# Routed experts of a two-layer model: second products two steps behind, the next expert's tokens turned inside the current expert

## The reference, cut to what matters

```python
xt = x.reshape(n, h)                       # n = 4096, h = 256
S = jax.nn.sigmoid(xt @ Wg).T              # 8 experts
G, I = jax.lax.top_k(S, k)                 # k = 1024 tokens for each expert
ex = xt[I]
hid = jax.nn.gelu(jnp.einsum('ekh,ehf->ekf', ex, W1) + b1[:, None, :], approximate=False)   # f = 1024
out = (jnp.einsum('ekf,efh->ekh', hid, W2) + b2[:, None, :]) * G[..., None]
new_x = jnp.zeros_like(xt).at[I.reshape(-1)].add(out.reshape(-1, h))
```

## Time and profile before

| | us |
|---|---|
| median of 3 runs | 4653.36 |
| lowest, highest | 4644.17, 4657.75 |
| profiled execution: its time | 4639.34 |
| profiled execution: span from first to last instruction | 4637.6 |
| stage `ae`, first `up` to last `down` | 416.79 |
| stage `ce`, the same | 420.58 |

### The profile page before, as it was taken

One profiled execution on the slowest core, in us unless ns is written; L12 is line 12 of the kernel. 1 busy time (PEld: TensorE's weight loads), 2 busy tenths in 40 slices (PEclk: granted clock), 3 DMA queues, 4 the chain that ended last, 5 costly groups with the idle time before them and its releaser, 6 DMA issues. The chain is left out here.

```text
span 4637.6 us, 74096 instructions
## 1 busy us (share of the span) xinstructions
PE 4047.9 (87%) x26222; PEld 3129.6 (67%) x26222; DVE 2729.8 (59%) x5268; ACT 1988.4 (43%) x3960; POOL 566.3 (12%) x428
## 2 busy tenths in 40 slices
PE   4599949989974599968999969999999997799999
PEld 3488835555544588857888856666566664788888
DVE  4544446665645544437777756655666555577777
ACT  1555524544440555512333336555655554133332
POOL 0144321211200144210000000000000000000000
PEclk6699968999995799969999979999999999699999
DMA  3243220000003343220000020000000001000001
GB/s 113 89 93 82 30 57 6 24 20 16 24 25 100 100 85 80 29 56 11 14 10 11 6 77 6 10 11 11 1 10 10 11 6 38 18 11 14 10 14 36
DMA packets 144876, 159.23 MB, mean 34 GB/s; under 512 B 20320, under 2 KB 132704, under 8 KB 144352
## 3 DMA queue, kind: packets, MB, share of 16 engines
q1 hardware_dynamic: 117728, 113.15, 7.5%
q0 software_dynamic: 26880, 42.48, 5.0%
HBM read 105.01 MB, written 50.59 MB: 34 GB/s over the span
## 5 line engine op out<-in xcount | busy, mean ns | idle before, releaser
L1895 ACT ACTIVATE e_prob<-e_s_ps,e_small 128x512 f32<-128x512 f32 x512 | 346.7, 685 | 173.2 <-PE e_t_ps L1785 88.2
L2006 DVE TENSOR_REDUCE e_small<-e_s_ps 128x2 f32<-128x1024 f32 x256 | 313.3, 1224 | 170.8 <-PE e_s_ps L1772 166.6
L1312 ACT ACTIVATE b_pt<-b_t_ps 128x1024 f32<-128x1024 f32 (+3 forms) x256 | 180.9, 706 | 305.0 <-PE b_t_ps L1244 304.0
L1785 PE MATMUL e_t_ps<-const,e_prob 128*128 128x128 f32 x2048 | 267.9, 274 | 9.5 <-ACT e_pt L1884 5.3
L1806 PE MATMUL e_z_ps<-e_pt,e_v 128*64 128x512 f32 x1024 | 275.5, 617 | 0.4 <-DVE e_zf L2086 0.4
L1984 POOL TENSOR_TENSOR e_wide<-e_small,const 128x512 f32<-128x512 f32 x64 | 66.5, 1039 | 1708.4 <-DVE e_small L2079 1708.4
L1785 PEld LDWEIGHTS e_t_ps<-const,e_prob 128*128 128x128 f32 x2048 | 234.1, 141 | 55.8 <-issue 22.5
L1495 DVE TENSOR_REDUCE b_small<-b_s_ps 128x2 f32<-128x1024 f32 (+3 forms) x256 | 209.8, 820 | 85.1 <-PE b_s_ps L1223 81.1
L942 DVE SCALAR_TENSOR_TENSOR d_xs<-d_o_ps,d_coef,d_xs 128x256 f32<-128x256 f32 x576 | 238.1, 476 | 1.3 <-PE d_o_ps L62 1.3
L942 DVE SCALAR_TENSOR_TENSOR f_xs<-f_o_ps,f_coef,f_xs 128x256 f32<-128x256 f32 x576 | 238.1, 476 | 1.3 <-PE f_o_ps L62 1.3
L60 PE MATMUL f_h_ps<-f_x_hi,f_w_hi 128*128 128x512 f32 x576 | 227.5, 395 | 0.0
(11 more groups left out here) (540 smaller groups left out, 11757.0 us busy)
## 6 DMA issues: line engine op xcount, KB each, us to landing
ae_raw<-w_dram SPq DMA_DIRECT2D x16, 1024.0 KB
ce_raw<-w_dram SPq DMA_DIRECT2D x16, 1024.0 KB
d_raw<-m_dram SPq DMA_DIRECT2D x54, 128.0 KB, 2.2
f_raw<-m_dram SPq DMA_DIRECT2D x54, 128.0 KB, 2.2
b_xs<-x_dram SPq DMA_DIRECT2D x9, 512.0 KB, 3.8
ar_xs<-x_dram SPq DMA_DIRECT2D x8, 512.0 KB, 9.3
x_dram<-ar_xs SPq DMA_DIRECT2D x8, 512.0 KB, 7.6
rows_dram<-ar_xn POOLq DMA_DIRECT2D x8, 512.0 KB, 4.7
```

What stands on the lines that cost most here:

```text
L1312: act.activation(pt[:, kt % 2, a, :, 0:width], t_ps[:, :, 0:width], ACT.Exp).then_inc(p_ready, 1)
L1785: last = pe.transpose(t_ps[:, h, kt * P:(kt + 1) * P], prob[:, bank_of(s) + h, kt * P:(kt + 1) * P], ident)
L1895: act.activation(prob[:, at], s_ps[:, at], ACT.Exp, bias=nmx[:, at:at + 1], accum_out=sums[:, buf, h * QT + s:h * QT + s + 1]).then_inc(p_ ...
L2006: dve.tensor_reduce(nmx[:, at:at + 2], s_ps[:, at:at + 2], AX.X, ALU.max, negate=True).then_inc(mx_ready, 1)
```

## The change

PE does `down(n-2)` after `up(n)`; the last two `down` of an expert stand inside steps 0 and 1 of the next. `h_hi` and `h_lo` get four buffers. `x_hi` and `x_lo` get a second buffer, and the next expert's transposes run in four parts behind steps 8, 10, 12 and 14, each followed by its splits on ACT and DVE. The weights are split in 8 pieces of double width behind steps 2, 3, 4, 5, 7, 9, 11 and 13. The fetches have a semaphore for each pair of tiles, and each half of `added` has its own. POOL issues the fetches of expert e+2 between the two scatters of expert e. `add_b2` and `scale_y` of the second half run at step 2 of the next expert, those of the first half at step 10. A stage starts when half of its first expert's tokens are turned; the other half is turned behind steps 0 and 2. The gates are copied out of `xg` at step 9 (`take_gates`).

```diff
+        LAG, RING = 2, 4
+        PAIRS = CC // 2
+        SPLIT_AT = (2, 3, 4, 5, 7, 9, 11, 13)
+        TURN_AT = (8, 10, 12, 14)
+        WS = len(SPLIT_AT)
+        WP = WCOL // WS
...
-        x_hi, x_lo = sb("x_hi", [P, KC, CAP], F32R), sb("x_lo", [P, KC, CAP], F32R)
+        x_hi, x_lo = sb("x_hi", [P, 2, KC, CAP], F32R), sb("x_lo", [P, 2, KC, CAP], F32R)
-        h_hi, h_lo = sb("h_hi", [P, 2, GTOK], F32R), sb("h_lo", [P, 2, GTOK], F32R)
+        h_hi, h_lo = sb("h_hi", [P, RING, GTOK], F32R), sb("h_lo", [P, RING, GTOK], F32R)
...
+            def gather_next(e):
+                gp.wait_ge(t_ready, e * PAIRS)
+                gp.wait_ge(gates_done, e)
+                gather(e)
+            def scatter(e, g):
+                gp.wait_ge(y_ready, e * HALF + g + 1)
+                if g == 0 and e > 0:
+                    for half_ in range(HALF):
+                        gp.wait_ge(added[half_], e * 16 * GT)
...
             gather(0)
+            gather_next(1)
             for e in range(E0):
-                body(e, e + 1 < E0)
+                scatter(e, 0)
+                if e + 2 < E0:
+                    gather_next(e + 2)
+                scatter(e, 1)
...
+            def transposes(e, j):
+                pe.wait_ge(gathered[j], e * 32 + 32)
+                if j >= 2 or later(e):
+                    pe.wait_ge(x_lo_done, e * PAIRS + (j - 1))
...
             def up(e, b, n):
                 g, f = divmod(n, FC)
+                if f == 0:
+                    pe.wait_ge(x_lo_done, e * PAIRS + PAIRS // HALF * (g + 1))
                 if n == 0:
-                    pe.wait_ge(x_lo_done, e * (CC // 2) + CC // 2)
-                    pe.wait_ge(w_lo_done, e * N + N)
-                if n >= 2 or not isinstance(e, int) or e > 0:
+                    pe.wait_ge(w_lo_done, e * WS + WS)
+                if n >= 2 or later(e):
                     pe.wait_ge(hid_ready, e * N + (n - 1))
...
             def body(e, b, more):
                 for n in range(N):
                     up(e, b, n)
-                    if n >= 1:
-                        down(e, b, n - 1)
-                if more:
-                    transposes(e + 1)
-                down(e, b, N - 1)
+                    if n >= LAG:
+                        down(e, b, n - LAG)
+                    elif later(e):
+                        down(e - 1, 1 - b, N + n - LAG)
+                    if isinstance(e, int) and e == 0 and n in (0, 2):
+                        transposes(0, 2 + n // 2)
+                    if more and n in TURN_AT:
+                        transposes(e + 1, TURN_AT.index(n))
...
             # scalar, in body(e, b, more), behind gelu(n)
+                    if n >= RING or later(e):
+                        act.wait_ge(w2_done, e * N + (n + 1 - RING))
+                    act.activation(h_hi[:, n % RING], hid[:, n % 2], ACT.Copy).then_inc(hid_hi, 1)
+                    if more and n in SPLIT_AT:
+                        split_w(e + 1, 1 - b, SPLIT_AT.index(n))
+                    if isinstance(e, int) and e == 0 and n in (0, 2):
+                        split_x(0, 0, 2 + n // 2)
+                    if more and n in TURN_AT:
+                        split_x(e + 1, 1 - b, TURN_AT.index(n))
+                    if n == LAG and later(e):
+                        scale_y(e - 1, 1 - b, 1)
+                    if n == FC + LAG:
+                        scale_y(e, b, 0)
...
             # vector, in body(e, b, more), behind h_lo(n): split_w, split_x as on scalar, then
+                    if isinstance(e, int) and e == 0 and n == 3:
+                        take_gates(0, 0)
+                    if n == LAG and later(e):
+                        add_b2(e - 1, 1 - b, 1)
+                    if n == FC + LAG:
+                        add_b2(e, b, 0)
+                    if more and n == FC + 1:
+                        take_gates(e + 1, 1 - b)
+            def take_gates(e, b):
+                for j in range(PAIRS):
+                    dve.wait_ge(gathered[j], e * 32 + 32)
+                if not isinstance(e, int) or e > 1:
+                    dve.wait_ge(y_ready, (e - 1) * HALF)
...
```

More of the change, by code:

```diff
@@ L437, in loads_of, with later, over_experts @@
         def loads_of(e, b):
-            return e * 8 + (8 if b else 16)
+            return 16 * (e // 2 + 1) if isinstance(e, int) else e * 8 + (8 if b else 16)
+        def later(e):
+            return not isinstance(e, int) or e > 0
+        def over_experts(eng, body):
+            body(0, 0, True)
+            with eng.Fori(0, E0 // 2 - 1) as i:
+                body(i * 2 + 1, 1, True)
+                body(i * 2 + 2, 0, True)
+            body(E0 - 1, 1, False)
         @block.sync
@@ L468, in gather @@
                     gp.indirect_dma_start(out=xg[:, c], out_offset=None, in_=rows,
[L469 to L481 removed]
+                                          in_offset=bass.IndirectOffsetOnAxis(ap=idx[:, e, c:c + 1], axis=0)).then_inc(gathered[c // 2], 16)
@@ L519, in down @@
                 pe.wait_ge(hid_lo, e * N + (n + 1))
-                if f == 0 and (not isinstance(e, int) or e > 0):
+                if f == 0 and later(e):
                     pe.wait_ge(y_sum, (e - 1) * HALF + (g + 1))
@@ L561, in body, with scale_y @@
+            def scale_y(e, b, g):
+                act.wait_ge(y_sum, e * HALF + (g + 1))
+                for t in range(GT):
+                    last = act.activation(y[:, g, t], y[:, g, t], ACT.Copy, scale=gates[:, b, g * GT + t:g * GT + t + 1])
+                last.then_inc(y_ready, 1)
             def body(e, b, more):
-                act.wait_ge(b1_in[b], (e // 2 + 1) * 16 if isinstance(e, int) else loads_of(e, b))
+                act.wait_ge(b1_in[b], loads_of(e, b))
                 for n in range(N):
@@ L577, in body @@
-                if more:
-                    split_x(e + 1)
-                scale_y(e, b, 1)
-            def scale_y(e, b, g):
-                act.wait_ge(y_sum, e * HALF + (g + 1))
-                if g == 0:
-                    act.wait_ge(gates_done, e + 1)
-                for t in range(GT):
-                    last = act.activation(y[:, g, t], y[:, g, t], ACT.Copy, scale=gates[:, b, g * GT + t:g * GT + t + 1])
-                last.then_inc(y_ready, 1)
-            for n in range(N):
-                split_w(0, 0, n)
@@ L639, in _ @@
-            for n in range(N):
-                split_w(0, 0, n)
-            split_x(0, 0)
-            dve.wait_ge(b2_in, 16)
-            body(0, 0, True)
-            with dve.Fori(0, E0 // 2 - 1) as i:
-                body(i * 2 + 1, 1, True)
-                body(i * 2 + 2, 0, True)
-            body(E0 - 1, 1, False)
+                    dve.tensor_tensor(h_lo[:, n % RING], hid[:, n % 2], h_hi[:, n % RING].bitcast(F32), ALU.subtract).then_inc(hid_lo, 1)
+                    if more and n in SPLIT_AT:
+                        split_w(e + 1, 1 - b, SPLIT_AT.index(n))
@@ L650 @@
+                    if more and n == FC + 1:
+                        take_gates(e + 1, 1 - b)
+            for m in range(WS):
+                split_w(0, 0, m)
+            for j in range(PAIRS // HALF):
+                split_x(0, 0, j)
+            dve.wait_ge(b2_in, 16)
+            over_experts(dve, body)
+            add_b2(E0 - 1, 1, 1)
 E1, TOPK, EG, TOPG = 16, 4, 4, 2
```

121 lines of the change are left out of this document (51 added, 70 removed).

## The result

The changed kernel takes 4540.76 us (median; 4536.31 to 4551.79), the kernel before 4655.56 us on the same chip: ratio 0.976, with 95% between 0.9734 and 0.9786. The forecast was 4568 in a range of 4554 to 4610. The direction was right; the gain is 115 us, where 86 was summed, and the time lies 13 us under the range.

The account below looks back on a forecast made before the run. PE's work plus its waits was taken to bound the two routed stages; with waits covered, ae gains 41.2 us and ce 44.6, so 4653.36 less 85.8 gives 4568 us, range 4554 to 4610.

Parts of the forecast that it names:

- the first 4 us: Start of each routed stage: matmuls run at the lower clock as before, taken as a loss of 2.1 us.
- Steps of 2.82 us: PE in each routed stage: 128 steps of one up and one down at 2.82 us, 361.0 us.
- boundaries without a wait: Between experts: nothing left of the 2.08 us wait for h_lo or the 0.98 us wait for x_lo.
- the start: Start of each routed stage: up(0) begins at 176.3 instead of 181.71 in ae, 5.0 us earlier in ce.
- The last 0.2 us of the sum: A final 0.2 us added to the sum for stage ae, given without a derivation.
- the pair of transposes: PE in each routed stage: 30 pairs at 0.59 us, 0.51 for transposes and 0.08 for the switch, 17.7 us.
- I take that along: Whole kernel: the 14.0 us between profiled execution and median stays after the change, giving 4568 in place of 4553.5.
- rival 1: ACT's chain is late at the thin places, giving back up to 22 us, perhaps clock drops too: 4588 us; chance 0.17.
- the thin places: ACT around steps 2 and 10, where scale_y precedes gelu: only 0.7 and about 1.2 us of room left.
- Rival 2: Jumps of PE's two-expert loop stall on instruction fetch, 8 us in all: 4576 us; chance 0.08.
- Rivals 3 and 4: Steps 8 to 14: late landings return part of the gain (4593 to 4613, 0.08) or all (4653, 0.03).
- Rival 5: Steps 8 to 14: spread transposes keep PE at the lower clock, making the kernel slower, 4825 us; chance 0.02.

Follow-up runs that it names:

- before_third: The kernel before, unchanged, profiled a third time on one of the faster chips: 4621.92 us in its profiled execution.
- late_before: The kernel before with four extra copies (2.1 us) on ACT ahead of the gelu of step 5 in every routed expert: 4675.1 us against 4618.36.
- lag_one: The changed kernel with the second products one step behind again in place of two: 4554.94 us, ratio 0.9857 to the kernel before.
- turn_at_end: The changed kernel with all four transposed parts behind step 15 again: 4567.93 us, ratio 0.9876 to the kernel before.
- through_half: The kernel before with the last down behind the next up(0), and each half of up(0) waiting only for its own tokens: 4587.52 us, ratio 0.9919.
- through: The kernel before with only the last down of an expert moved behind the next expert's up(0): 4618.08 us in one execution.
- late_after: The changed kernel with four extra copies (2.1 us) on ACT ahead of the gelu of step 5: 4548.19 us, ratio 0.985 to the kernel before.
- fetch_first: The kernel before with POOL's fetches of expert e+2 moved ahead of the second scatter of e: 4667.59 us in one execution.
- before_fifth: The kernel before, unchanged, profiled a fifth time on another chip of the slower kind: 4646.19 us in its profiled execution.

## Why the prediction was right, and where it was wrong

**Right: what bounds the stage.** It was costed as PE's work with no wait left, and that is what the windows show: 376.36 of 376.36 us busy, granted clock 1.00 behind the first 4 us. Those cost 2.0 us (the first expert's 46.92, less 16 x 2.82 and 6 x 0.44, and 2.86 for the two `down` that it does not hold), where 2.1 were put down. Steps of 2.82 us, boundaries without a wait and the start (`ae` 5.5 us earlier, predicted 5.4; `ce` 5.3, predicted 5.0) came as summed. The last 0.2 us of the sum have no row behind them and change nothing.

**Wrong in size: the pair of transposes.** The term was 30 x 0.59 = 17.7 us per stage, 0.51 for the transposes of a pair and 0.08 for the switch. A pair adds 3.17 + 2.91 - 2 x 2.82 = 0.44 to its two steps: 0.35 from the first transpose (223.04) to `up` (223.39), and 0.09 in the switch (0.32 to the next matmul, where 0.23 is usual). The switch was right, the transposes were not. I had read eight of them off the row behind a wait, which lasts 1.25 us and gives way after 1.01; the other row, with no wait in front, lasts 1.04 and has the next work behind it later, so it shows no such distance. By the rows after, a group's last 0.25 us (0.60 less 0.35) overlap what follows, and 1.04 less 0.25 is 0.79 for eight, 0.40 per pair. The difference is 30 x 0.15 = 4.5 us per stage, 9 in both, and an expert of 46.88 us in place of 47.5.

**Wrong: "I take that along".** This is the step that put the time outside the range. The sum against the profiled execution came to 4553.5; I added the 14 us by which the median lay above it, as if they belonged to the rest of the program. No execution near that median was profiled on the first chip, so where they lay is an estimate. In the five profiles of the kernel before, all that is not `ae` or `ce` takes 3749 to 3755 us, on either kind of chip; a median of 4655.56 then leaves 901 to 906 us for the two stages, where the profiled execution had 886.3. They are also what differs between the chips: on the two chips of the slower kind the kernel before has these stages at 441.3 and 445.0 us in one profile and at 449.2 and 447.8 in the other; where no gelu is late they are 434.2 and 434.1 (`before_third`). The last two pairs differ by 28.6 us, the medians of their chips by 33 (4651 and 4618): nearly the whole difference lies in these stages. After the change they are 395.3 to 395.5 in both profiles of it. Its median is that of its profiled execution on the first chip (4540.76 and 4541.68) and 7.9 us above it on the second, so the rest of the program has a scatter of its own. 4568 less 14 less 9 is 4545; the last 4 us are within that scatter.

A late gelu stood in the prediction only as a danger to the new kernel (rival 1), where it was really a gain: 2.1 us of lateness cost the kernel before 1.86 us in its step and most often a stretch at the lower clock (`late_before`), and the changed one's stages nothing. Where no gelu is late the change brings 81 us (4623.38 to 4541.95), with them 115. That 81 is near the 85.8 of the sum is luck in part: the sum started from a profile whose stages were 18 us longer than those of `before_third`, and it made the kernel after 9 us too long by the transposes. The prediction had found the late gelu "in the middle of looped experts", by the idle time of ACT, 3.52 us, where the gelu is 2.46 us behind the end of its `up`; what it lacked was to ask whether the scatter comes from there.

**Right for another reason: the wait at a boundary.** The prediction let the lag of two steps close the 2.08 us. `lag_one` costs 0.45 us per expert, `turn_at_end` 1.4, both 1.5. The other 2.7 are gained by `through_half`: the last `down` behind the next `up(0)`, and `up(0)` waiting for half of the tokens only. The first edit needs the second: `through` alone moves the wait to `x_lo` (1.58 us) and gives 0.9. The lag of two, worth little where ACT is on time, should be what makes the kernel safe against a late ACT; I did not run a late ACT with a lag of one, so this is argued from the order of work.

**The rivals.** Rival 1 (ACT late at the thin places): no `down` waits at `up(5)` or `up(13)`. In the looped experts a gelu is 2.7 us late at steps 3 and 11, behind `scale_y`, and the room left before `up(5)` and `up(13)` is 0.7 and 1.0 us, where 0.7 and 1.2 were summed; the 2.1 us of `late_after` at step 5 cost the stages nothing. Rival 2 (jumps): all middle experts take 46.88 us, those ahead of a jump and those behind it. The Trainium skill ("Runtime: NRT & Kernel Launch", section "Instruction fetch mechanics") has a taken branch out of the fetched window stall; no run here shows such a stall. Rivals 3 and 4 asked for waits that the list above does not have; the fetches are on time. Rival 5 (the transposes keep PE at the lower clock): granted clock 1.00 in both stages behind their first 4 us, with four transposes in every second step from 8 to 14. The rule of the Trainium skill ("TensorE: Matmul & The Clock Gate", section "Part 4: PE-mode transpose"), that a transpose does not count as PE's work in the way a matmul does, changes nothing here, where 5.6 us of matmuls stand between two groups of them.

**Open.** What makes gelu start 1 us or more after its `up` when a run of indirect fetches ends (1.0 to 2.7 us in the kernel before, up to 5.1 in `fetch_first`), whether PE's signal or ACT is late, and why on two chips of five. PE's own matmuls go on meanwhile until they need `h_lo`. Open too is why the lower clock in `late_before` comes at a boundary.

## What to carry to other kernels

The distance between the profiled execution and the median is part of what is to be explained: if it comes from the stage that the change mends, it can go with the change. So profile the kernel before twice, ask which stage differs, and whether its waits would be covered afterwards. At a boundary of a pipeline, try first which consumer waits for more than it needs (half of the tokens were enough) and whether a finished product can stand behind the next start; that gave the largest part of the gain per expert here (2.7 of 4.1 us), and the second alone gave 0.9. A chain that fills a step to 0.4 us should get slack even where the profile shows no wait, because lateness from outside costs its wait, and here most often a stretch at the lower clock too.

## What the runs showed of the hardware

- The same kernel differs by some 30 us between chips (4618 to 4625 against 4651 to 4656). Between `before_fifth` and `before_third`, 28.6 of 33 us lie in the two stages in which gelus start 1.0 to 2.7 us after their `up` has ended, near the last of a run of indirect fetches on POOL, and in which 10 stretches of 3.4 us at the lower clock stand in place of 4.
- 2.1 us of lateness on ACT cost 3.4 us in most experts: 1.86 in the step itself, and 1.5 because the granted clock stands at its lower level for 3.4 us behind the wait at the boundary, not behind the late step. The same boundary wait of 2.1 us is followed by no such stretch in most experts of the kernel before.
- Four transposes of 128x128 between a `down` and an `up` lengthen their steps by 0.44 us, the switch included: 0.11 us for each.
